# Routed experts of a mixture: 48 looped slots of one expert, or 32 unrolled slots of two experts with copied, stationary weights

## The reference

```python
logits = x @ gate_w
topk_ids = jnp.argmax(logits, axis=-1)
scores = jax.nn.sigmoid(jnp.max(logits, axis=-1))[:, None]
order = jnp.argsort(topk_ids)
sorted_x = (x * scores)[order]
g = ragged_dot(sorted_x, routed_gate_w, tokens_per_expert)   # [2048, 256]
u = ragged_dot(sorted_x, routed_up_w, tokens_per_expert)
d = ragged_dot(jax.nn.silu(g) * u, routed_down_w, tokens_per_expert)
return shared_out + d[inv_order]
```

## Time and profile before

| what | value |
|---|---|
| runs shown | 857.32 us median of 3, 855.09 to 857.62 |
| profiled execution, its own time | 864.35 us |
| its span, first to last instruction | 862.6 us |
| mean granted TensorE clock | 0.904 |
| instructions | 14653 |
| PE busy | 673.0 us, 78% of the span |
| DVE, ACT, POOL busy | 536.9, 375.7, 382.8 us |

### The profile page before, as it was taken

How to read it: one execution, slowest core, us unless ns; L and a number is a source line. 1 busy time by engine, 2 the same in 40 slices (tenths; PEclk the granted TensorE clock), 3 DMA queues, 4 the chain that set the end, 5 groups by cost and what they waited for, 6 DMA issues and landing times.

```text
span 862.6 us, 14653 instructions
## 1 busy us (share of the span) xinstructions
PE 673.0 (78%) x5076; PEld 405.6 (47%) x5078; DVE 536.9 (62%) x915; ACT 375.7 (44%) x602; POOL 382.8 (44%) x318
## 2 busy tenths in 40 slices
PE   3466788999898989989987554779898977788881
PEld 2244555566565656656665232124233444455551
DVE  7746668788887888888773356966763554122222
ACT  0112333665646565564645532254546621233330
POOL 3535457657575756757640164200000107265552
PEclk9667989999999999999999966689989888899996
DMA  8103200100100010010000038636326101122224
GB/s 247 27 13 106 84 15 20 25 14 19 27 16 18 20 25 21 13 27 20 14 14 1 0 106 152 138 101 144 108 79 232 50 1 42 46 62 60 61 61 117
DMA packets 35509, 50.59 MB, mean 59 GB/s; under 512 B 5966, under 2 KB 24698, under 8 KB 34170
## 3 DMA queue, kind: packets, MB, share of 16 engines
q1 hardware_dynamic: 33401, 45.58, 20.6%
q0 software_dynamic: 2048, 4.21, 1.4%
HBM read 30.31 MB, written 11.83 MB: 49 GB/s over the span
## 4 chain that ended last, share of the span: by engine, by line
PE 56%; DVE 15%; issue 14%; DMA 7%; ACT 4%; POOL 3%; SPq 1%; POOLq 0%; DVEq 0%; ACTq 0%
PE ps L1603 6%; PE ps L1397 5%; PE ps L1337 4%; PE ps L1328 4%; PE ps L1351 3%; PE ps L1294 3%; PE ps L1300 3%; PE ps L1295 3%; PE ps L1370 3%; PE ps L1461 3%; PE ps L1405 3%; DVE mneg L1139 3%; PE ps L1308 2%; DVE region_b L885 2%; PE ps L1616 2%
## 5 line engine op out<-in xcount | busy, mean ns | idle before, releaser
L567 POOL TENSOR_TENSOR rnorm<-ssum_c,neg_half 128x16 f32<-128x16 f32 x32 | 121.1, 3785 | 99.8 <-DVE ssum_c L935 99.8
L579 POOL TENSOR_TENSOR region_r<-region_b,region_d 128x512 f32<-128x512 f32 x64 | 112.4, 1776 | 61.8 <-DVE region_b L940 61.4
L1139 DVE TENSOR_REDUCE mneg<-ps 128x2 f32<-128x1024 f32 x64 | 75.3, 1217 | 36.4 <-PE ps L1532 36.4
L813 ACT ACTIVATE region_r<-ps 128x1024 f32<-128x1024 f32 x64 | 64.6, 1023 | 58.4 <-PE ps L1545 58.3
L545 POOL TENSOR_TENSOR var_eps<-mv,eps 128x4 f32<-128x4 f32 x20 | 4.0, 200 | 175.1 <-DVE mv L878 175.1
L670 POOL DMA_INDIRECT y_dram<-region_r x48 | 50.0, 1042 | 43.5 <-DVE region_r L1231 26.4
L1337 PE MATMUL ps<-ident,region_b 128*128 128x128 f32 x256 | 36.1, 286 | 42.3 <-DVE region_b L992 23.2
L1222 DVE TENSOR_TENSOR region_r<-region_r,ps 128x256 f32<-128x256 f32 x48 | 20.2, 421 | 77.4 <-ACT region_r L845 48.4
L699 ACT ACTIVATE region_a<-ps 128x1024 f32<-128x1024 f32 x32 | 32.8, 1025 | 77.9 <-PE ps L1295 77.9
L1603 PE MATMUL ps<-region_a,region_r 128*128 x96 | 55.3, 658 | 13.1 <-issue 12.5
L684 ACT ACT_TABLE_LOAD x49 | 62.9, 1283 | 1.6 <-PEq L1745 0.7
(11 more groups left out here) (214 smaller groups left out, 1589.4 us busy)
## 6 DMA issues: line engine op xcount, KB each, us to landing
region_a<-in_wgu SPq DMA_DIRECT2D x16, 512.0 KB, 3.6
region_b<-region_a SPq DMA_DIRECT2D x56, 130.0 KB, 2.3
region_d<-in_wd SPq DMA_DIRECT2D x4, 1024.0 KB, 6.0
xs_dram<-region_a SPq DMA_DIRECT2D x1, 3354.0 KB, 13.2
pts<-xs_dram SPq DMA_DIRECT2D x50, 64.5 KB
parts_dram<-region_b SPq DMA_DIRECT2D x8, 384.0 KB, 2.6
region_b<-parts_dram SPq DMA_DIRECT2D x6, 384.0 KB, 6.8
region_d<-in_wqkv SPq DMA_DIRECT2D x2, 768.0 KB, 9.2
```

The costliest lines, as they stand in the source:

```text
L567: g.tensor_tensor(rnorm[:, :], ssum_c[n % 2][:, :], neg_half[:, :], ALU.pow).then_inc(S["rnormed"], 1)
L579: g.tensor_tensor(dst, src, tab, ALU.mult).then_inc(S["rot_bb"], 1)
L813: act_(dst, bank(l1_bank[what, b, i], of=2), ACT.Exp).then_inc(T["ex"], 1)
L1139: d.tensor_reduce(mneg[b % 2][:, 2 * i:2 * i + 2], bank(l1_bank[what, b, i], of=2) .rearrange("p (q t) -> p q t", q=2), AX.X, ALU.max, neg ...
```

## The change

The padded list now begins every expert at a multiple of 64 rows (`HALF`), at most 63 half slots, which are taken two at a time: 32 slots (`PAIRS`) of 128 rows, each with two halves that may belong to two experts. All is unrolled. The weights of both experts of a slot are copied from `wgu` and `wd` to one of three fixed buffer pairs (`w_pair`), the first expert's by VectorE, the second's by ACT (two instructions each, of 512 and of 256 columns). The expert numbers are now read by VectorE's and ACT's sequencers. In `gate_up` the 128x128 weight blocks are stationary and 64 token columns stream past, eight matmuls for a slot; the result is already transposed, so `gated_T` and `back_sb` go. In `down` the 64 columns of `act_r` are stationary and the two experts write partitions 0 to 63 and 64 to 127 of one bank, four matmuls for a slot. The routing arrays grow from 512 to 1024 and from 1664 to 2048 elements.

```diff
-SLOT_TILES = TILES + EXP - 1
-LOOP_TILES = -(-SLOT_TILES // AHEAD) * AHEAD
+HALF = P // 2
+HALVES = TOK // HALF
+PAIRS = -(-(HALVES + EXP - 1) // 2)
+AHEAD, NUM, WBUF = 4, 2, 3
...
+            def weights_two(j, e):                       # ACT
+                need(a, M["y_mm"], j - WBUF + 1)
+                dst = w_pair[j % WBUF][1]
+                act_(dst[:, 0:2 * INTER], wgu[:, bass.ds(e, 1), :].rearrange("p a n -> p (a n)"), ACT.Copy)
+                act_(dst[:, 2 * INTER:EW], wd[:, bass.ds(e, 1), :, :].rearrange("p a c n -> p (a c n)"), ACT.Copy)\
+                    .then_inc(M["w_two"], 1)
...
+            for j in range(PAIRS):                       # ACT
+                if j + 2 < PAIRS:
+                    weights_two(j + 2, e)
+                if j + 3 < PAIRS:
+                    e = expert_two(j + 3)
+                if j + 1 < PAIRS:
+                    gate_sb(j + 1)
+                if j + 2 < PAIRS:
+                    tokens_sb(j + 2)
...
-            link(d.tensor_tensor(m1.rearrange("p (e k) -> p e k", e=EXP), cnt.unsqueeze(2).to_broadcast([P, EXP, TILES]),
+            link(d.tensor_tensor(over, cnt.unsqueeze(2).to_broadcast([P, EXP, HALVES]),
...
+            for j in range(PAIRS):                       # VectorE
+                if j + 2 < PAIRS:
+                    weights_one(j + 2, e)
+                if j + 3 < PAIRS:
+                    e = expert_one(j + 3)
+                if j + 1 < PAIRS:
+                    gated(j + 1)
+                routed_sb(j)
...
-            def gate_up(t, i, e):
-                pe.wait_ge(M["xT_sb"], i * AHEAD + t + 1)
-                mm(bank(2 + t % 2), xsT[t % 2], wgu[:, bass.ds(e, 1), :].rearrange("p a n -> p (a n)"),
-                   start=True, stop=True).then_inc(M["gu_mm"], 1)
+            def gate_up(j):
+                pe.wait_ge(M["xT_sb"], j + 1)
+                pe.wait_ge(M["w_one"], j + 1)
+                pe.wait_ge(M["w_two"], j + 1)
+                for w in range(2):
+                    for c in range(2 * IC):
+                        at = c * P + w * HALF
+                        last = mm(bank(2 + j % 2)[:, at:at + HALF], w_pair[j % WBUF][w][:, c * P:(c + 1) * P],
+                                  xsT[j % 2][:, w * HALF:(w + 1) * HALF], start=True, stop=True)
+                last.then_inc(M["gu_mm"], 1)
...
+            def down(j):
+                pe.wait_ge(M["r_act"], j + 1)
+                need(pe, M["y_sb"], j - 1)
                 for c in range(IC):
+                    for w in range(2):
+                        at = c * P + w * HALF
+                        last = mm(bank(6 + j % 2)[w * HALF:(w + 1) * HALF, 0:P], act_r[j % 2][:, at:at + HALF],
+                                  w_pair[j % WBUF][w][:, 2 * INTER + c * P:2 * INTER + (c + 1) * P], start=(c == 0),
+                                  stop=(c == IC - 1), skip_group_check=True)
                 last.then_inc(M["y_mm"], 1)
...
+            pe.wait_ge(M["x4s"], BATCH)
+            tokens_T(0)
+            tokens_T(1)
+            gate_up(0)
+            for j in range(PAIRS):
+                if j + 1 < PAIRS:
+                    gate_up(j + 1)
+                if j + 2 < PAIRS:
+                    tokens_T(j + 2)
+                down(j)
```

More of the change, by code:

```diff
@@ L212, in build @@
         act_r = [region_r[:, 6400 + i * INTER:6400 + (i + 1) * INTER] for i in range(2)]
-        actT = [region_r[:, 6912 + i * INTER:6912 + (i + 1) * INTER] for i in range(2)]
         ys = [region_r[:, 7424 + i * P:7424 + (i + 1) * P] for i in range(AHEAD)]
@@ L218, in build @@
         ntile, incl, base_e = (region_b[:, 8704 + i * EXP:8704 + (i + 1) * EXP] for i in range(3))
-        exp_of_f = region_b[0:1, 8800:8800 + LOOP_TILES + AHEAD]
-        exp_of = region_b[0:1, 8864:8864 + LOOP_TILES + AHEAD].bitcast(I32)
+        exp_of_f = region_b[0:1, 8800:8800 + 2 * PAIRS]
+        exp_of = region_b[0:1, 8880:8880 + 2 * PAIRS].bitcast(I32)
+        EW = 2 * INTER + IC * P
+        w_pair = [[region_b[:, at:at + EW] for at in two] for two in ((0, EW), (6144, 6144 + EW), (9344, 4112))]
         xs_dram = nc.dram_tensor("xs_dram", (SLOT_ROWS, ROW), FP).ap()
@@ L253, in build @@
             "rank_mm", "slots", "scaled", "up_mm", "silu", "acted", "down_mm", "x4s", "scattered",
-            "sp_turn", "pool_turn", "ids", "xT_mm", "xT_sb", "gu_mm", "r_silu", "r_act", "actT_mm", "actT_sb", "y_mm", "y_sb", "x4")}
+            "w_one", "w_two", "ids", "xT_mm", "xT_sb", "gu_mm", "r_silu", "r_act", "y_mm", "y_sb", "x4")}
         xs_in = [sem(f"moe_xs_in{i}") for i in range(AHEAD)]
@@ L258, in build @@
         block = ctx.enter_context(nc.Block())
[L260 to L269, removed]
         def l1_steps():
@@ L498, in _ @@
                 sp.dma_start(rows_in[r], xs_dram[r * P:(r + 1) * P, :]).then_inc(xs_in[r], 16)
-            def refill(t, j):
+            for j in range(PAIRS - AHEAD):
                 sp.wait_ge(M["xT_mm"], j + 1)
-                if not isinstance(j, int):
-                    sp.sem_inc(M["sp_turn"], 1)
                 sp.wait_ge(M["ids"], j + 1)
[L506 to L516, removed]
+                sp.dma_start(rows_in[j % AHEAD], xs_dram[(j + AHEAD) * P:(j + AHEAD + 1) * P, :]).then_inc(xs_in[j % AHEAD], 16)
             for r in range(AHEAD):
-                sp.wait_ge(ys_out[r], 16 * PASSES)
+                sp.wait_ge(ys_out[r], 16 * (PAIRS // AHEAD))
             for b in range(BATCH):
@@ L525, in _ @@
                 sp.dma_start(rows, xr[:, b * NT:(b + 1) * NT, :]).then_inc(S["stored"], 16)
-            for r in range(AHEAD):
-                sp.wait_ge(xs_in[r], 16 * (PASSES + (r < NUM)))
             sp.wait_ge(S["stored"], 16 * BATCH)
@@ L646, in _, with number @@
                                      in_=rows_m[:, t, :], in_offset=None).then_inc(M["scattered"], 16)
[L648 to L653, removed]
-                                ALU.max).then_inc(M["ids"], 1)
[L656 to L669, removed]
+            def number(j):
+                pool.wait_ge(xs_in[j % AHEAD], 16 * (j // AHEAD + 1))
+                if j >= AHEAD:
+                    pool.wait_ge(ys_out[j % AHEAD], 16 * (j // AHEAD))
+                g.tensor_scalar(slot_id[:, j % AHEAD:j % AHEAD + 1], rows_in[j % AHEAD][:, P:ROW], float(j % AHEAD), None,
+                                ALU.max).then_inc(M["ids"], 1)
+            for j in range(NUM):
+                number(j)
+            for j in range(PAIRS):
+                if j + NUM < PAIRS:
+                    number(j + NUM)
+                pool.wait_ge(M["ids"], j + 1)
+                pool.wait_ge(M["y_sb"], j + 1)
                 g.indirect_dma_start(out=y_dram[:, :],
-                                     out_offset=bass.IndirectOffsetOnAxis(ap=slot_id[:, r:r + 1], axis=0),
-                                     in_=ys[r], in_offset=None).then_inc(ys_out[r], 16)
-            experts(pool, pool_step)
+                                     out_offset=bass.IndirectOffsetOnAxis(ap=slot_id[:, j % AHEAD:j % AHEAD + 1], axis=0),
+                                     in_=ys[j % AHEAD], in_offset=None).then_inc(ys_out[j % AHEAD], 16)
         @block.scalar
@@ L836, in tokens_sb, with gate_sb @@
+            def tokens_sb(j):
                 a.wait_ge(M["xT_mm"], j + 1)
[L837 to L841, removed]
+                need(a, M["gu_mm"], j - 1)
+                act_(xsT[j % 2], bank(j % 2)[:, 0:P], ACT.Copy).then_inc(M["xT_sb"], 1)
+            def gate_sb(j):
                 a.wait_ge(M["gu_mm"], j + 1)
-                if not (isinstance(j, int) and j < 2):
-                    a.wait_ge(M["r_act"], j - 1)
-                act_(silu_r[t % 2], bank(2 + t % 2)[:, 0:INTER], ACT.Silu).then_inc(M["r_silu"], 1)
@@ L847, in back_sb @@
[L847 to L863, removed]
+                need(a, M["r_act"], j - 1)
+                act_(silu_r[j % 2], bank(2 + j % 2)[:, 0:INTER], ACT.Silu).then_inc(M["r_silu"], 1)
+            a.wait_ge(M["slots"], 2)
+            a.wait_ge(M["x4s"], BATCH)
+            a.wait_ge(M["w_gu"], 16 * 16)
+            a.wait_ge(M["w_d"], 4 * 16)
+            e = expert_two(0)
@@ new lines, in _ @@
+            weights_two(0, e)
+            e = expert_two(1)
+            tokens_sb(0)
+            weights_two(1, e)
+            e = expert_two(2)
+            tokens_sb(1)
+            gate_sb(0)
+            for j in range(PAIRS):
[7 more added lines that the diff above has]
+                    tokens_sb(j + 2)
@@ L1216, in _, with expert_one, weights_one, gated @@
                 add_s(b)
-            def gated(t, j):
+            def expert_one(j):
+                return v.value_load(exp_of[0:1, 2 * j:2 * j + 1], min_val=0, max_val=EXP - 1)
+            def weights_one(j, e):
+                need(v, M["y_mm"], j - WBUF + 1)
+                dst = w_pair[j % WBUF][0]
+                d.tensor_copy(dst[:, 0:2 * INTER], wgu[:, bass.ds(e, 1), :].rearrange("p a n -> p (a n)"))
```

(54 more changed lines are left out.)

27 lines of the change are left out of this document (11 added, 16 removed).

## The result

The changed kernel takes 906.96 us (median of 4 runs, 904.34 to 911.78) against 856.31 us before (4 runs, 855.09 to 857.62): a ratio of 1.0589, 95% interval 1.0558 to 1.062. The forecast was 896, its range 845 to 908. The profiled executions are 911.78 and 864.35 us, 47.4 us apart, with spans of 909.8 and 862.6.

A forecast was written before the change was run, and what follows sets the result against it. TensorE bounds the routed-expert stage; at 1.2 GHz, 740.9 + first gate_up 3.4 + 31 x 4.6, then last down and write, ends at 889.6 against 850.68: +38.9 on 857.3 gives 896 us, range 845 to 908.

The forecast's parts named there:

- stays low: Routed stage: TensorE's clock stays at 1.2 GHz throughout, as the array waits for weight blocks; chance 0.72.
- the change of width: After down, the next full-width instruction starts later: 0.1 us added at 1.2 GHz, bounds nothing or 0.4 a slot.
- The rival of a rising clock: Routed stage: clock rises as it does now, 2.7 us a slot, -19 us, 838 us; chance 0.19.
- The rivals' turning point: Routed stage: above 3.3 us a slot the kernel is slower at any mixture of clock levels.
- the thin stretches of the earlier trace: Before the routed stage: mostly 34-column matmuls at 686.8 to 690.2 us, then clock 0.50; taken as nearest evidence.
- The slot: TensorE at 1.2 GHz: gate_up 3.42, transpose 0.21, down 0.86, width change 0.1, together 4.6 us; 4.9 with gaps of 0.4.
- At 2.4 GHz: Slot at the high clock: gate_up 1.79 plus 0.89 for the chain over ACT, 2.7 us.
- The chain over ACT: gate_up(j+2) awaits the token copy behind silu: tail 0.16, hand-over 0.04, silu 0.26, copy 0.28, restart 0.15 us.
- The copies: Expert weights per slot: ACT 0.60 and 0.39 us, VectorE 1.95 for both; hidden behind TensorE's 4.6 us.
- The start: Longer routing arrays, number read and copies: first gate_up near 740.9 instead of 740.0; up to 2.0 us on x4s.
- The end: Last down waits 0.2 and takes 1.0 us; last write ends 1.5 us after the last matmul, giving 3.9 back.
- The level of the runs: Median of the runs taken 7.0 us below the profiled execution, so 857.3 + 38.9 = 896 us.

The follow-up runs named there:

- the second experiment: Changed kernel plus 18 wide filler matmuls (bf16, into an unused bank) once, before slot 9's gate_up, none at the start: 859.4 us in one run.
- the third experiment: Changed kernel whose down keeps all 128 columns of act_r stationary for either expert, in two banks (full slots): 845.32 us, ratio 0.9875 to the kernel before.
- the eighth experiment: Changed kernel without fillers, only the first six slots with the full-width down, the others paired: 840.91 us, ratio 0.9823 to the kernel before.
- the first experiment: Changed kernel plus 18 wide filler matmuls (14 and 4) in TensorE's idle time before the first slot: 835.65 to 839.66 us (three executions), 902.87 and 905.73 (two).
- the sixth experiment: Changed kernel with fillers (22 and 4), six full-width slots then paired ones, tokens_T and its copy before gate_up and silu: 836.04 us, ratio 0.9765 to before.

## Why the prediction was right

**The level of the clock**, on which the sign hung: as predicted, 0.50 to the end. The change took the wide streams away with which the old stage had come back to 1.00, and the thin ones did not bring it back. That the clock makes the difference, and that what went before decides it, is shown by the second experiment. The reason given for "stays low", that in `gate_up` the array waits for blocks, is not shown. For it speak the third and the eighth experiment, in which a fuller `down` raises the clock, in all eight executions. But they also take the change of width away with its pauses, and no run did one without the other. Against the pauses as the cause speaks that the first 32 instructions of `gate_up` in the third experiment follow each other without any, and the clock is 0.50 beside them.

The rival of a rising clock had 2.7 us a slot, near the 2.64 measured at 1.00. A clock that rises by itself, which gave its 838 us, was seen in no execution of the changed kernel; the 835.65 to 839.66 of the first experiment were bought with fillers. The rivals' turning point, 3.3 us a slot, lies between the measured 2.64 and 4.87. One thing said beside it misled: the thin stretches of the earlier trace rows ended in a fall from the higher level, while the new slots hold it in three traces. What makes the difference between them was not varied in a run. The forecast of "stays low" needed only that the stage starts at 0.50.

**The slot, 4.6 us predicted, 4.83 to 4.88 measured.** `gate_up` took 3.48 us where 3.42 was predicted. What was sized too low is the change of width, 0.1 taken: the trace shows 0.35 from the transpose to `down` instead of 0.21, and 1.05 for `down` instead of 0.86, together 0.33. I had named 0.4 as the upper bound, and 4.9 us a slot with it.

**At 2.4 GHz**, 2.7 predicted, 2.64 measured. The chain over ACT that I summed does release `gate_up` in the second experiment's trace. But the sum left out the change of width at this clock, and by the sixth experiment it costs the same time when the chain is gone. The number came out for one of two reasons that end together.

**The copies** are hidden, as predicted; VectorE's two take 0.42 and 0.29 us where the bound taken was 1.95 together, since the nearest row stood at its slow end.

**The start**: 740.11 against 740.9 predicted. VectorE's longer routing steps moved the last add by 1.06 us (it ends at 738.04 instead of 736.98), where up to 2.0 had been taken. From there to the first `gate_up`, which waits for ACT's copy of the tokens, it is 2.07 us, where 2.0 had been taken.

**The end**: the last `down`s take 2.12 us together (893.33 to 895.45), where 1.2 was predicted for one and its wait. The last write ends 2.3 us after the last matmul (897.78), where 1.5 was predicted. The write before it starts 0.75 us behind its copy, and the sum had some 0.2 for that; the last one also waits for the one before.

**The sum.** The last write came 8.2 us later than computed (897.8 against 889.6): 7.0 from 31 steps of 4.83 instead of 4.6 us, 0.2 from the last `gate_up`, 0.9 from the last `down`s and 0.8 from the write, less 0.8 at the start.

**The level of the runs.** The forecast took the runs 7.0 us below the profiled execution, and they lie 4.8 below it. With the 8.2 us this is most of the 11 us by which 896 was too low: the change cost 50.7 us between the medians and was put at 38.9. The other executions were not traced, so where in the kernel they differ is not known. The 907 us lie 1 us inside the upper end of the range. That end is only 2 us above what the bound of 4.9 us a slot gives, so it is partly luck that the time fell inside it.

## What to carry to other kernels

Before making weights stationary, compare the columns that stream past a block with the time that the block's load takes: with 64 fp32 columns TensorE is busy all the time and its array is not (at 2.4 GHz a step takes 0.11 us with 32, 64 or 128 columns, so that with 64 it streams for half of it at most). Such a stage can have two stable speeds (here 4.87 and 2.64 us a slot), and which one it gets depends on what TensorE did before it; look at the granted clock of the stage, not at its busy share. Of the two remedies, wide fillers in front of the paired slots helped in three of five executions; with full slots, the first six or all, none of sixteen executions stayed low, with or without fillers. The version with six full slots is the one to use without fillers; with them and with the tokens' earlier copy it ran in 836.04 us, 2.35% under the kernel before.

## What was not expected of the hardware

The same sequence of instructions ran at 2.64 us a slot and at 4.87, a factor of 1.84, in one execution, with 18 wide matmuls between. A program with fillers in front of the stage took 835.65 us in one execution and 905.73 in another. In the one traced the clock fell behind a wait of 2.29 us, and in the kernel before it held behind one of 2.61, with the same four fillers behind it; the matmuls that follow are thin in one and wide in the other, and no run shows whether that decides. A `down` that takes 0.65 us more at 1.2 GHz made the kernel 62 us faster. And the pause at the change from 64 to 128 stationary columns, 0.17 us at 2.4 GHz, is there with nothing to wait for. The Trainium skill says that changing the tiling mode drains TensorE (TensorEngine Tiling (Array Packing), Key Properties), and this pause agrees with it.
